# Four indirect scatters of a chunk: from a group of adding ones to plain ones spread over the next substitution

## The reference

```
# part 1: attention by the delta rule, 4 heads, dk = 128, dv = 32
delta_t = (v_t - k_t^T S_{t-1}) * beta_t ;  S_t = S_{t-1} + k_t delta_t^T ;  o_t = q_t^T S_t
x = layernorm(x + (rmsnorm(o) * norm_w * silu(g)) @ Wo)
# part 2: mixture of 8 experts, the best 2 of each token, capacity 640 rows per (batch row, expert) here
combined_mask = (count <= capacity)          # what comes after the 640th row is dropped
dispatch      = einsum('bsm,bsec->ebcm', hidden_states, dispatch_mask)
expert_out    = einsum('ebch,ehm->ebcm', silu(h1) * h3, w2)
x = layernorm(x + final)
```

## Time and profile before

| | us |
|---|---|
| median of 3 runs | 583.95 |
| lowest and highest of them | 579.88, 586.90 |
| the profiled execution, its own time | 586.65 |
| its span, first to last instruction | 584.9 |

### The profile page before, as it was taken

How to read it: one execution, slowest core, us unless ns; L and a number is a source line. 1 busy time by engine, 2 the same in 40 slices (tenths; PEclk the granted TensorE clock), 3 DMA queues, 4 the chain that set the end, 5 groups by cost and what they waited for, 6 DMA issues and landing times.

```text
span 584.9 us, 18665 instructions
## 1 busy us (share of the span) xinstructions
PE 499.9 (85%) x6852; PEld 394.7 (67%) x6852; DVE 335.1 (57%) x1304; ACT 328.8 (56%) x901; POOL 392.4 (67%) x689
## 2 busy tenths in 40 slices
PE   6659999999898989998987982299999999999910
PEld 4435666666565666665655561299999999999910
DVE  5114377775675666676767775246545545645434
ACT  3333767676567655765764363155555555555466
POOL 2454468888888888888888745227677667757750
PEclk9975999999999999999998597599999999999975
DMA  3675327634442444244333324415465455454357
GB/s 86 170 194 154 108 30 131 92 35 46 52 53 30 49 53 54 31 52 53 43 36 48 48 29 99 103 45 102 55 121 104 55 116 101 54 103 52 32 101 215
DMA packets 137060, 45.81 MB, mean 78 GB/s; under 512 B 89488, under 2 KB 131472, under 8 KB 136976
## 3 DMA queue, kind: packets, MB, share of 16 engines
q1 hardware_dynamic: 114656, 29.60, 24.3%
q0 software_dynamic: 20736, 9.51, 18.4%
q10 hardware_dynamic: 1584, 5.59, 2.5%
HBM read 21.13 MB, written 23.55 MB: 76 GB/s over the span
## 4 chain that ended last, share of the span: by engine, by line
PE 41%; POOL 35%; issue 12%; DMA 6%; DVE 2%; ACT 2%; SPq 1%; POOLq 1%; ACTq 0%; DVEq 0%
PE ps L854 17%; POOL slots_in L1480 13%; PE ps L868 12%; POOL xs L1467 10%; POOL prod L1466 9%; PE ps L830 2%; POOL silu L1487 2%; ACT xTs L1112 1%; PE ps L616 1%; POOL Vk L1493 1%; DMA a_diag<-A 1%; PE ps L587 1%; DMA inv<-xs 1%; PE ps L601 1%; PE ps L609 1%
## 5 line engine op out<-in xcount | busy, mean ns | idle before, releaser
L1510 POOL DMA_INDIRECT x_store<-xk,row x80 | 125.1, 1564 | 71.7 <-ACT xk L1075 52.2
L1480 POOL DMA_INDIRECT slots_in<-x,slot x64 | 101.1, 1580 | 28.8 <-issue 18.1
L1466 POOL TENSOR_TENSOR prod<-a,xs 64x15 f32<-64x15 f32 (+7 forms) x240 | 72.4, 302 | 52.1 <-DVE xs L1243 34.5
L1358 DVE TENSOR_TENSOR hb<-ps,hs 128x320 f32<-128x320 f32 (+1 forms) x128 | 63.0, 492 | 55.5 <-ACT hs L1067 53.3
L1467 POOL TENSOR_TENSOR xs<-xs,prod 64x15 f32<-64x15 f32 (+7 forms) x240 | 65.9, 274 | 18.8
L1067 ACT ACTIVATE hs<-ps 128x320 f32<-128x320 f32 (+1 forms) x128 | 55.9, 436 | 36.0 <-PE ps L854 27.3
L868 PE MATMUL ps<-w2s,hb 128*128 128x128 f32 x640 | 74.1, 275 | 0.0
L854 PE MATMUL ps<-xeTh,w13h 128*128 128x320 f32 x224 | 71.5, 319 | 1.7 <-DVE xeTl L1385 1.7
L868 PEld LDWEIGHTS ps<-w2s,hb 128*128 128x128 f32 x640 | 72.8, 192 | 0.0
L854 PE MATMUL ps<-xeTh,w13l 128*128 128x320 f32 x224 | 70.0, 312 | 0.0
L854 PE MATMUL ps<-xeTl,w13h 128*128 128x320 f32 x224 | 69.9, 312 | 0.0
(11 more groups left out here) (188 smaller groups left out, 1011.2 us busy)
## 6 DMA issues: line engine op xcount, KB each, us to landing
slots_in<-zeros ACTq DMA_DIRECT2D x10, 520.0 KB, 4.0
xe<-slots_in SPq DMA_DIRECT2D x16, 325.0 KB
w<-w_in SPq DMA_DIRECT2D x8, 448.0 KB
xTs<-xT SPq DMA_DIRECT2D x4, 512.0 KB, 5.5
a_diag<-A SPq DMA_DIRECT2D x64, 32.0 KB
inv<-xs SPq DMA_DIRECT2D x16, 128.0 KB
xi<-inv SPq DMA_DIRECT2D x16, 128.0 KB
xk<-x SPq DMA_DIRECT2D x4, 512.0 KB, 5.6
```

The source lines that it names most:

```text
L1358: v.tensor_tensor(hb[rows_, par, c, HALF * g:HALF * g + HALF], ps[rows_, at, 0:HALF], hs[rows_, s % 4, :], ALU.mult).then_inc(h_ready, 1)
L1466: link(g.tensor_tensor(pr_, bc(a16[:, j + 1:, j], 2, j + 1), bc(xs[:, 0, j, 0:j + 1], 1, m), ALU.mult))
L1480: g.indirect_dma_start(out=xs_d[:, :], out_offset=bass.IndirectOffsetOnAxis(ap=to, axis=0), in_=x1[:, p % 2, j, k, :], in_offset=None, com ...
L1510: g.indirect_dma_start(out=x1_d[:, :], in_=ye[:, par, i, :], in_offset=None, out_offset=bass.IndirectOffsetOnAxis(ap=row[:, par, i:i + 1], ...
```

## The change

The four DMAs of a chunk lose `compute_op`, so they write plainly. They are no longer sent as a group after Vk: `send_rows(p, i)` sends one, and `solve(n)` calls it ahead of the rows j = 1, 4, 8 and 12 of its substitution, for chunk n - 4 (it was chunk n - 3, after the substitution of n). In the steps after the last substitution (p of 16 and more) the four of chunk p - 4 are sent in a row, ahead of the silu. The wait for `slot_ready` stands at the first of the four.

```diff
+SEND_AFTER = (1, 4, 8, 12)
+SEND_BACK = 4
+            def send_rows(p, i):
+
+                if i == 0:
+                    pool.wait_ge(slot_ready, p + 1)
+                    if p == 0:
+                        pool.wait_ge(xs_zero, 16 * (XS_ZEROS + 1))
+                    apart(pool)
+                j, k = i // TOPK, i % TOPK
+                g.indirect_dma_start(out=xs_d[:, :], in_=x1[:, p % 2, j, k, :], in_offset=None,
+                                     out_offset=bass.IndirectOffsetOnAxis(ap=slot[:, p % 2, i:i + 1], axis=0)
+                                     ).then_inc(scat[p % 2], 16)
+
             def solve(n):
 
                 pool.wait_ge(c2_out, n + 1)
                 for j in range(15):
                     m = 15 - j
+                    if j in SEND_AFTER:
+                        at(send_rows, n - SEND_BACK, SEND_AFTER.index(j))
...
-            def scatter(p):
-
-                pool.wait_ge(slot_ready, p + 1)
-                if p == 0:
-                    pool.wait_ge(xs_zero, 16 * (XS_ZEROS + 1))
-                apart(pool)
-                for j in range(2):
-                    for k in range(TOPK):
-                        to = slot[:, p % 2, 2 * j + k:2 * j + k + 1]
-                        g.indirect_dma_start(out=xs_d[:, :], out_offset=bass.IndirectOffsetOnAxis(ap=to, axis=0),
-                                             in_=x1[:, p % 2, j, k, :], in_offset=None, compute_op=ALU.add
-                                             ).then_inc(scat[p % 2], 16)
...
             for p in range(NP + LAST):
                 at(solve, p)
+                if p >= NP:
+                    for i in range(2 * TOPK):
+                        at(send_rows, p - SEND_BACK, i)
                 at(scaled_values, p)
-                at(scatter, p - 3)
                 at(silu_of, p - 1)
```

## The result

| | before | after |
|---|---|---|
| median of 12 runs each | 584.03 us | 594.23 us |
| lowest and highest | 579.88, 593.01 | 588.57, 597.47 |
| profiled execution, its span | 584.9 | 590.7 |

The ratio is 1.0156, with a 95% interval of 1.0113 to 1.0198: slower by 1.6%. The prediction was 600 us in a range of 572 to 622.

The account below looks back on a forecast made before the run. POOL's own work was taken to bound part 1 at 20.00 us a step, PE second at about 18.5. Substitutions with sends +23.7, after the last -5, last four sends -2.8: +15.9, so 600 us, range 572 to 622.

Parts of the forecast that it names:

- The cover of the store's round trip: Between substitutions: Vk, scatters and silu hide 3.65 us; with the scatters moved, POOL idles 2.35 us a step.
- c: POOL's time on one plain send: 1.05 us, estimated as two thirds of an adding scatter's 1.57.
- the gap g ahead of a send: From the subtraction's end to the send's start in the substitution: taken as 0.70 us, ends 0.16 and 0.76.
- the rival of the hidden start: POOL prepares each of 48 sends while the subtraction runs: gap 0.16, 574 us, at PE's bound 561; chance 0.22.
- x: What each of four sends adds to a substitution, gap plus POOL time less 0.03: 1.72 us; even at 1.30.
- the tail: After the last substitution, z_32 of chunk 15 comes about 5.5 us after the copy, before 11.0: a gain of 5.
- nothing changes from z_32 on: Behind the last chunk's z_32, times were to stay as in the kernel before.
- The last four: Last chunk's four sends, from slots to landing: 7.7 us in place of 10.52, a gain of 2.8.
- the start: Chunk 4's substitution, the first with sends, starts at 94.28 in place of about 96.03: 1.75 us gained once.
- Plain as dear as adding: Rival on POOL's sends: a plain one costs 1.57 us like an adding one; 627 or 608 us; chance 0.20.
- The writer that takes half the time for a plain send: Even rival: POOL's time goes by reads alone, a plain send takes 0.78; +1.8, 586 us; chance 0.16.

Follow-up runs that it names:

- e2: Kernel before with plain DMAs, still sent as a group at the old place behind Vk: 560.37 us, ratio to before 0.9524.
- e3: Kernel after with two buffers for a16 and xs, so scaling waits for the solution and store one chunk further back: 574.82 us, ratio to before 0.9814.
- e1: Kernel after with adding DMAs, so only the place of the sends differs from the kernel before: 623.57 us, ratio to before 1.0627.
- e4: Kernel after without the nop ahead of the first of four sends: 590.27 us, ratio to before 1.0036.
- e10: e2 run again, the kernel before with plain DMAs as a group at the old place: 564.04 us, ratio to before 0.9616.
- e8: Kernel after with 5 matmuls of unused result where PE waits for the last chunk's inverse: 592.47 us, ratio to before 1.0108.
- e7: Kernel after with two of four plain sends inside the substitution (rows 1 and 8) and two behind Vk: 585.03 us, ratio to before 1.0007.
- e6: Kernel after with 12 matmuls of unused result where PE waits for the last chunk's inverse: 606.63 us, ratio to before 1.0381.
- e5: e2 with the two buffers and early waits of e3: 644.85 us, ratio to before 1.1023.

## Why the prediction came out right

**The mechanism held, point by point.** The bound of part 1 was POOL's own work, with PE close behind: e2 takes 0.55 us from each send, and the step stops at 18.3 with PE full. The cover of the store's round trip went: 3.65 us were worked out from two places of the trace before, 3.66 were measured, and an idle time of 2.35 was forecast, 2.40 measured. e3 takes most of that wait away and e1 keeps it. The plain send was put at c = 1.05, an estimate of two thirds of the adding one; the trace has 1.03. That POOL's time counts accesses, the reason given for the two thirds, no run shows. The time itself is the weaker evidence: a range of 50 us also held "no change", and errors of both signs offset each other in it.

**The term that was mis-sized is the gap g ahead of a send.** I took 0.70 from the nearest wait; measured are 0.81 for the first and 0.28 for the three others, 0.41 in the mean. The row at 341.38 had a nop between wait and scatter, and e4 shows that a nop costs 0.33. The four sends add 5.8 us and not 6.9, and the step is 20.6 and not 21.7. The two gaps of 0.16 and 0.30 that I had set aside were nearer. So the rival of the hidden start was half right: three sends of four came within 0.12 of its g, but with the first one's 0.81 the step still came out above 20.00.

**The parts of the sum.** The last copy ends at 334.79, 7.9 us later than before; 23.7 was forecast, 15.8 more. Of that, 12.6 are the sends: the twelve substitutions took 203.5 us, which makes x = 1.46 and not 1.72. (The gap alone would make 48 x 0.29 = 14; other instructions ran a little longer than alone.)

The other 3.2 are luck. Chunk 3's copy ended 3.3 us earlier than before (83.95 against 87.21), ahead of any send, and from there chunk 4 started as forecast (7.11 us on, 7.07 forecast). It is not the change's doing: e2 and e10 are the same kernel, and there this copy ends at 83.76 and at 87.57. What differs is PE's clock from 44 to 60 us, here before and after:

```profile
44.00:60.00 16.00, 16.00 (x136) 8.85 (x136) 7.26 (x25) 6.46 (x16) 7.72 (x27) 0.57 0.52 137
```

```profile
44.00:60.00 16.00, 14.71 (x178) 9.27 (x178) 7.37 (x25) 8.37 (x21) 9.11 (x31) 0.89 0.64 179
```

In e2 it is 0.89 as well, in e10 0.57. Without these 3.3 us the spans would differ by 9.1, close to the 10.2 of the medians.

**A term with the wrong sign was the tail.** I counted a gain of 5 us between the last copy and the last slots. Before, they are 34.5 us apart, after 35.7. The first half came out in number: z_32 of the last chunk came 6.5 us after the copy (5.5 expected), 4.5 sooner than before. The reason given for it did not. In the kernel before PE didn't stand behind the silu; it had work, at a low clock:

```profile
327.00:338.00 11.00, 9.95 (x99) 6.95 (x100) 8.84 (x35) 3.27 (x11) 7.54 (x6) 0.66 0.52 62
```

And e2 and e10, with the group in its old place, have z_32 7.0 and 6.8 us after the copy. The timeline of the kernel after, all engines:

```profile
341.32 1.05 PE L634 MATMUL ps<-xh,A 32*32 32x16 f32 x64 [4.94 <-DVE xh L1176]
```

But PE had waited for it for 4.94 us. From 341 to 357 its clock then stood at 0.50, and "nothing changes from z_32 on" was wrong by 5.7 us. In the kernel before a low spell of the same kind lay ahead of z_32, in e8 too. So the 4.5 gained and the 5.7 lost fit one low spell in two places. That is argued from the windows; whether the change moved the spell, or only these two executions differ, is not shown.

**The last four** went as said: 7.2 us from the slots to the landing (7.7 forecast, 10.52 before).

```profile
375.04 2.65 DMA slots_in<-x,slot
```

That row is from the chain of waits of the kernel after; the landing itself is 0.8 us shorter than in the earlier trace rows.

Together: +7.9, +1.2 in the tail and -3.3 at the end are the +5.8 of the spans. The forecast of +15.9 was too high because one error of 12.6 (the sends), one of 3.2 (the start, luck) and 0.5 at the end outweighed the 6.2 of the tail, on the other side.

**The rivals.** Plain as dear as adding is refuted (1.03 against 1.58). The writer that takes half the time for a plain send would give 0.78; the trace has 1.03. That rule came from a division of labour which the Trainium skill's page "GPSIMD Engine Reference" states (when to use GPSIMD), and no run here shows it; if it holds, reads alone don't set the time. The Trainium skill's page "DMA: Bandwidth & Descriptors" (anatomy of one DMA) calls descriptor generation small. Here an indirect DMA of 128 rows takes 1.03 us of POOL. Without it x would be near 0.4; with it x is 1.46, and a step comes out even at 1.30. So it decided the sign.

## What to carry to other kernels

When an engine looks full from end to end, ask what its work covers: a cheap operation that stands over a round trip (store, landing, rescale) costs nothing there, and its whole price once it is moved into the chain the round trip starts from. Try the two halves of an edit apart: here plain DMAs are worth 4 to 5% and their new place costs more than that. A wait that is freed is not free of effect either; time it, in the company it will have. And before you explain a difference between two profiled executions by the change, hold their clocks side by side, and two executions of one kernel too: 3.3 us here were neither kernel's.

## What the runs showed of the hardware

- An indirect DMA of 128 rows of 520 bytes took POOL 1.58 us where it added and 1.03 us where it wrote.
- The gap ahead of such a DMA was 0.28 us behind a small operation that it waits for; with a nop and another semaphore 0.81, without the nop 0.48.
- Two DVE instructions of 64x16 elements took 0.62 and 0.65 us and ended just behind a plain indirect DMA of POOL and with POOL's silu (e7, ten steps of eleven). In the kernel before they took 0.16 and 0.17, beside adding scatters too. What makes the difference is open.
- PE's clock was at half of full speed (1.2 of 2.4 GHz) for 16 us after PE had waited 4.94 us; with matmuls in that place it was at full behind them (e6, e8), but in e8 a low spell of 19 us had just ended. Waits of 4.5 us in one and the same place were followed by 3 us at half clock in one execution and by 19 in another. The same 344 matmuls took 29 us at a mean clock of 0.68 and 23 at 0.92 to 0.94.
- Two executions of one kernel (e2, e10) reached the same copy at 83.76 and 87.57 us, with a mean clock of 0.89 and 0.57 from 44 to 60 us.
- With early waits, DVE and ACT stood still for about 4 us, seven times each in 200 us, with no releaser in the profile (e5). The cause is open.
